# Moving the half node sums in front of a 64-row filter layer in a graph-network kernel

## What is computed

```python
h    = relu(layernorm(x))                               # 6250 x 128
xw   = h @ W_in
W_ij = (softplus(f_ij @ W_f1 + b_f1) - ln2) @ W_f2 + b_f2   # f_ij: 200000 x 20, W_f1: 20 x 128
x_ij = xw[dst] * (W_ij * cutoff)                        # one message per edge
out  = segment_sum(x_ij, src, 6250)                     # sums by source node
x    = x + (softplus(out @ W_o1 + b_o1) - ln2) @ W_o2 + b_o2
```

## Time and profile before

| what | value |
|---|---|
| median of three runs | 2415.03 us |
| the profiled execution | 2413.26 us, of which its span 2411.4 us |
| PE busy | 2207.1 us (92%), weight loads 1401.0 us |
| DVE busy | 1898.1 us (79%) |
| ACT busy | 1775.7 us (74%) |
| POOL busy | 1855.0 us (77%) |
| mean granted TensorE clock | 0.981 of full |
| HBM traffic | 98 GB/s over the span |

### The profile page before, as it was taken

How to read it: one execution, slowest core, us unless ns; L and a number is a source line. 1 busy time by engine, 2 the same in 40 slices (tenths; PEclk the granted TensorE clock), 3 DMA queues, 4 the chain that set the end, 5 groups by cost and what they waited for, 6 DMA issues and landing times.

```text
span 2411.4 us, 56737 instructions
## 1 busy us (share of the span) xinstructions
PE 2207.1 (92%) x16842; PEld 1401.0 (58%) x16842; DVE 1898.1 (79%) x3929; ACT 1775.7 (74%) x4145; POOL 1855.0 (77%) x1192
## 2 busy tenths in 40 slices
PE   1689999999999999999999999999999999999945
PEld 1566566566656656665665666566566656656623
DVE  8677877877787787878778777877887887788758
ACT  1578777777777777777777777777777777777713
POOL 2288888888887888788788888878887887888853
PEclk9899999999999999999999999999999999999968
DMA  9265556555555555555555555555555555555565
GB/s 354 100 99 91 88 88 90 87 88 88 90 87 87 90 89 88 88 90 87 87 89 87 89 89 90 86 87 91 86 89 88 89 86 88 90 87 88 81 162 180
DMA packets 351511, 239.84 MB, mean 99 GB/s; under 512 B 89459, under 2 KB 338497, under 8 KB 351071
## 3 DMA queue, kind: packets, MB, share of 16 engines
q0 software_dynamic: 164000, 77.47, 33.4%
q1 hardware_dynamic: 185987, 158.25, 24.1%
q10 hardware_dynamic: 1212, 0.42, 0.1%
HBM read 139.86 MB, written 96.12 MB: 98 GB/s over the span
## 4 chain that ended last, share of the span: by engine, by line
PE 71%; DMA 8%; issue 7%; DVE 5%; POOL 4%; ACT 4%; ACTq 0%; SPq 0%; POOLq 0%; DVEq 0%
PE ps L1289 20%; PE ps L1308 16%; PE ps L1268 11%; PE ps L1258 8%; PE ps L1275 8%; DMA acc<-region,target 7%; PE ps L1340 4%; POOL acc L598 4%; PE ps L1266 3%; ACT region L729 1%; ACT region L753 1%; ACT region L711 1%; ACT region L713 1%; DMA w_f<-in_L_gnn_W_f_dram 1%; DMA region<-in_x_dram 0%
## 5 line engine op out<-in xcount | busy, mean ns | idle before, releaser
L598 POOL DMA_INDIRECT acc<-region,target x1132 | 1797.1, 1588 | 424.5 <-issue 274.9
L1289 PE MATMUL ps<-region 128*128 128x386 bf16 x3024 | 650.0, 336 | 66.5 <-ACT region L729 46.6
L729 ACT ACTIVATE region<-ps 128x386 bf16<-128x386 f32 x756 | 372.3, 492 | 272.5 <-PE ps L1289 217.2
L1308 PE MATMUL ps<-region 64*128 64x448 bf16 x4536 | 497.8, 352 | 9.5 <-DVE region L1046 9.5
L1289 PEld LDWEIGHTS ps<-region 128*128 128x128 bf16 x3024 | 253.4, 97 | 367.6 <-issue 169.8
L1011 DVE SCALAR_TENSOR_TENSOR region<-ps,bf_negative,region 128x512 f32<-128x512 f32 x391 | 292.1, 747 | 210.3 <-ACT region L715 119.2
L753 ACT ACTIVATE region<-ps,cut_col 128x128 f32<-128x128 f32 x1564 | 439.0, 362 | 0.7 <-PE ps L1340 0.7
L1268 PEld LDWEIGHTS ps<-w_f,region 128*128 128x128 f32 x3128 | 414.7, 193 | 11.2
L1268 PE MATMUL ps<-w_f,region 128*128 128x128 f32 x3128 | 415.4, 276 | 0.0
L711 ACT ACTIVATE region<-ps,bf 128x512 f32<-128x512 f32 x391 | 268.6, 687 | 71.2 <-PE ps L1258 11.5
L1275 PEld LDWEIGHTS ps<-region 128*128 128x128 f32 x2264 | 294.0, 191 | 26.2 <-DVE region L1011 4.0
(11 more groups left out here) (128 smaller groups left out, 1700.0 us busy)
## 6 DMA issues: line engine op xcount, KB each, us to landing
dst_b<-dst_rows SPq DMA_DIRECT2D x391, 128.0 KB
src_b<-src_rows SPq DMA_DIRECT2D x283, 128.0 KB
acc<-region,target POOLq DMA_INDIRECT x1132
attrT<-in_edge_attr_dram SPq DMA_DIRECT2D x782, 20.0 KB
acc<-region SPq DMA_DIRECT2D x20, 640.0 KB, 17.4
xwin<-xw_parts SPq DMA_DIRECT2D x391, 31.5 KB
region<-acc SPq DMA_DIRECT2D x48, 256.0 KB, 4.5
xw_parts<-parts SPq DMA_DIRECT2D x12, 384.0 KB, 2.3
```

The lines of the kernel that those rows point to most:

```text
L598: nc.gpsimd.indirect_dma_start(out=acc[a], out_offset=bass.IndirectOffsetOnAxis(ap=target[:, slot, t:t + 1], axis=0), in_=summed[:, slot, ...
L729: nc.scalar.activation(binned[:, h, j, :], binned_ps[:, 0:PC], ACT.Copy).then_inc(s_binned, 1)
L1289: ins = MM(binned_ps[:, 0:PC], place[:, h % 2, t, j * P:(j + 1) * P], payload_high[:, h % 2, t, :], start=(t == 0), stop=(t == T - 1))
L1308: ins = MM(ps[6 + r][:, 0:NL], binned[rows, slot, j, part * F:(part + 1) * F], in_node[rows, sums_until(kk, i) % 2, slot, :], start=(d == ...
```

## The change

`w_f1` and `attrT` get all 128 partitions. DVE clears both at its start, and tells of it with a new semaphore `s_blank`; ACT waits for the first before it loads `W_f1`, SP for both before it first loads `attrT`. The loads still bring 20 rows each, so 44 rows of each half stay zero. `hidden_product` now contracts over 64 rows. And in PE's step the call of `add_nodes` goes from behind `filter_product` to just ahead of the wait for, and the call of, `hidden_product`. Nothing changes on the other engines after the set-up, nor in the schedule.

```diff
-        w_f1 = sb("w_f1", [64 + RBF, F])
+        w_f1 = sb("w_f1", [P, F])
...
-        attrT = sb("attrT", [64 + RBF, 4, CE // 2])
+        attrT = sb("attrT", [P, 4, CE // 2])
...
+        s_blank = sem("rows_past_the_rbf_cleared")
...
+            sp.wait_ge(s_blank, 2)
             for c in range(2):
                 load_attr(c, c)
...
+            act.wait_ge(s_blank, 1)
             for r in range(2):
                 act.dma_start(w_f1[64 * r:64 * r + RBF, :], W_f1).then_inc(s_w, 16)
...
             V.memset(ones_bf[:, :], 1.0)
+            V.memset(w_f1[:, :], 0.0).then_inc(s_blank, 1)
+            V.memset(attrT[:, :, :], 0.0).then_inc(s_blank, 1)
             dve.wait_ge(s_iota, 3)
...
                 for r in range(2):
-                    rows = slice(64 * r, 64 * r + RBF)
+                    rows = slice(64 * r, 64 * r + 64)
                     ins = MM(hidden_ps[:, r, :], w_f1[rows, :], attrT[rows, slot, :], start=True, stop=True)
...
                     for kk, h, i, late in jobs:
                         if not late:
                             bin_up(kk, h, i)
+                    for job in sums_at.get(k, ()):
+                        add_nodes(*job)
                     n = k + 1
                     if exists(n) and n > 0:
                         after_slot(pe, s_attr, n, 2)
...
                         filter_product(n % 2)
-                    for job in sums_at.get(k, ()):
-                        add_nodes(*job)
                     for kk, h, i, late in jobs:
                         if late:
                             bin_up(kk, h, i)
```

## The result

The changed kernel takes 2774.11 us (median of 4 runs, 2772.3 to 2776.74) against 2415.34 us before (median of 4 runs). The ratio estimated over the runs is 1.1492, 95% interval 1.1475 to 1.1509; the two medians alone give 1.1485. The forecast was 2749 us, with a range of 2690 to 2830: the time lies inside it, 25 us above the forecast.

What follows compares the result with a forecast made beforehand. Full steps were taken as bound by PE's own work. Circles of waits add 234 + 75, less small corrections, +305, and clock loss +29, to 2413.3 profiled: 2747, median 2749 us; range 2690 to 2830.

Steps and rivals of the forecast that it cites:

- Path one: Circle from hidden product through ACT, DVE's addition to accT and node sums: 6.91 us per OLD step, +234 us.
- the rival with DVE's order: Only the early-bins circle binds, because something lets DVE add sooner: +152, 2567 us; chance 0.05.
- Path two: Early bins wait for ACT to take out late bins: 6.06 us per step with a NEW half, +75 us.
- PE's work: Joining node sums and hidden product on PE saves 0.28 us, to 5.41 us a step.
- The rival in which the blocks don't join: On PE, 64-row hidden halves don't overlap or the passage stays: up to +160, some 2900 us; chance 0.04.
- The drain rule: Fewer tiling-mode changes on PE make a pure gain: 103 us off PE, POOL capping at 2342 us; chance 0.03.
- The clock: Longer PE waits lower the granted clock in half of 52 OLD steps without same_product: 26 x 1.12 = 29 us.
- Set-up: Two clears on DVE, estimated 0.1 and 0.9, covered by its wait for POOL: cost 0, at most 1.
- What the marks said: Profile signs: 62 steps in 400 us, 175 us addition waits, PE under 85%, more POOL waits, bins waiting for ACT.

Runs made afterwards that it cites:

- e3: The changed kernel with DVE's addition to accT moved from behind the previous step's message to just ahead of combine: 2555.8 us, ratio 1.0588.
- e10: As e3, and on ACT the late bins are taken out ahead of the gathered rows, not behind them: 2418.9 us against 2413.6, ratio 1.0019.
- e1: The changed kernel with add_nodes put back behind filter_product, hidden product still at 64 rows: 2412.1 us against 2413.7, ratio 0.9992.
- e2: The kernel before with add_nodes moved ahead of the hidden product, which stays at 20 rows: 2842.4 us, ratio 1.1791.
- e4: The changed kernel with add_nodes right behind the 64-row hidden product, ahead of gather and filter: 2350.4 us, ratio 0.9739.
- e5: As e4, add_nodes right behind the hidden product, but the hidden product stays at 20 rows: 2375.5 us, ratio 0.984.
- e9: The changed kernel with matmuls nobody reads in the two waits of the 52 OLD steps without same_product: 2748.1 us, ratio 1.138.

## Why the prediction was right, step by step

- **Path one.** 6.91 us was forecast for an OLD step, 7.00 measured. The term that was short is the release: 0.05 from line 729 to the bins, taken over for the addition, where the changed kernel's timeline has 1210.36 - 1210.21 = 0.15 (0.12 to the first weight load), and so in all 186 cases. The kernel before had shown it: its 6 waits for the addition ended 0.15 behind it too. 0.09 x 184 = 17 us of the 25 that the forecast was low. e3 takes this path away and OLD steps fall to the 6.07 of the others; the rival with DVE's order is answered the other way: it could add sooner, but only where its line is moved.
- **Path two.** 6.06 was forecast, from the one kind of step in the earlier trace rows that had no node sums; 6.07 measured, and e10 shows by ACT's order that this is its cause.
- **PE's work.** 0.28 us less a step: the changed kernel has 0.21 of it between the joined blocks (1.68 for 1.89); the passage from the filter is the rest (0.98 for eight matmuls ahead of the node sums in the earlier trace rows, 1213.38 - 1212.49 = 0.89 ahead of the bins now). That 64 rows cost the same as 20 was an estimate; e1 shows it. The rival in which the blocks don't join (0.04) is out by e2 and by the 1.68.
- **The drain rule.** The Trainium skill (TensorEngine Tiling (Array Packing), Key Properties) says that a change of the tiling mode drains TensorE. The runs agree in the effect: e4 against e5 is 25 us, the changed kernel against e2 68 us, for one passage fewer a step; they don't part a drain from a weight load that couldn't run ahead. As a forecast this rule alone would have had the sign wrong, because the passages were only in PE's work and the move was in everybody's order.
- **The clock.** 26 losses at 1.12 us, 29 us, were forecast; 25 stretches were recorded, 24 of them in the 52 steps it named. Each cost more: in the 24 OLD steps 1.06 (8.07 for the 7.01 of the same steps at full clock), and the NEW step behind it another 0.46, since the stretch ran into it. That is 36 us, the other 7 of the 25. The agreement in the count is luck in good part: "half of them" rested on two cases in the earlier trace rows, and both of those had the one wait of 1.40, not the pair; e2 with the same pairs of waits has 11 stretches, 5 of them in such steps. That the waits are the cause is shown by e9, where no filled step lost the clock, and by e3, where without the second wait none did.
- **Set-up.** 0 forecast, and e1 has none. The clears took 0.17 and 0.91 us (0.1 and 0.9 estimated), and DVE's next instruction starts at 3.14 us, as before (3.13).
- **What the marks said.** 61 steps in 400 us (62 forecast), 178.8 us of waits for the addition (175), PE at 81% (under 85%), and POOL's waits for DVE's targets went from 81.6 to 462.8 us. 321 weight loads of bins waited for ACT, where nearly every step was forecast.

## What to carry to other kernels

In a pipeline written out by hand, the price of moving a block on one engine need not lie in that engine's work: follow each wait of the moved block round to itself (who starts it, what that one waits for) and add up the durations; the longest circle is the new step if it is longer than the work of the busiest engine. A step of the old kernel that happens to lack the cover shows the length of such a circle before anything is changed. And if two blocks are to stand side by side, try both orders: here the block on which the others wait had to come first (2350.4 us against 2774.1).

## What was not expected

- The granted clock fell without a long idle time. Two waits of 1.40 and 0.88 us with 0.86 of matmuls between them were followed by half clock in 24 of 52 steps, and filling them with matmuls whose result nobody reads won 26 us in e9. The wait of 1.40 alone, 52 times in e3, was never followed by it there; near the start of the loop of before it was once, in one of the two cases of the earlier trace rows.
- The release of an engine by a semaphore was not one number here. From ACT's line 732 to the early bins the changed kernel's trace has 0.05 or 0.06 us in 107 cases and 0.14 in 46 (the bins at 1208.70 are one), from DVE's addition to the node sums 0.15. The 46 are all a chunk's first tile of bins, which waits for three semaphores (`s_pay`, `s_place`, `s_binned`) where the others wait for one; a node sum that starts a group also waits for more than one. So the longer time goes here with the number of waits rather than with the engine that releases; that this is the cause is not shown, since no run changes that number alone.
